# A feed-forward tail woven on VectorE: gate products between the quantiser's steps, a pass moved to ScalarE, a lag of three groups

## The reference

```python
x = x + attention(_layernorm(x), ln_gamma, ln_beta, w_qkv, w_out, b_out)   # 16 heads of 64, rotary, softmax
def fp4_quant_dequant(x):            # blocks of 16 along the last axis
    scale = max(abs(xb)) / 6.0;  scale = maximum(scale, 1e-12)
    xn = xb / scale
    q = GRID[searchsorted(MID, abs(xn))] * sign(xn) * scale     # GRID 0 .5 1 1.5 2 3 4 6
def fp4_linear(x, w): return fp4_quant_dequant(x) @ fp4_quant_dequant(w).T
y = _layernorm(x)
h = silu(fp4_linear(y, w_gate)) * fp4_linear(y, w_up)
x = x + fp4_linear(h, w_down)
```

## Time and profile before

| engine | busy us | share of the span |
|---|---|---|
| TensorE | 1506.3 | 95% |
| GpSimd | 1353.2 | 85% |
| VectorE | 1155.6 | 73% |
| ScalarE | 896.9 | 56% |

### The profile page before, as it was taken

One profiled execution on the slowest core, in us unless ns is written; L12 is line 12 of the kernel. 1 busy time (PEld: TensorE's weight loads), 2 busy tenths in 40 slices (PEclk: granted clock), 3 DMA queues, 4 the chain that ended last, 5 costly groups with the idle time before them and its releaser, 6 DMA issues.

```text
span 1588.7 us, 25645 instructions
## 1 busy us (share of the span) xinstructions
PE 1506.3 (95%) x9257; PEld 789.0 (50%) x9257; DVE 1155.6 (73%) x1562; ACT 896.9 (56%) x1383; POOL 1353.2 (85%) x793
## 2 busy tenths in 40 slices
PE   3799999999999999999999999999999999998677
PEld 1345555455555555545545454555545445554455
DVE  4777777677777777777777777777777777764687
ACT  1266566665665665756656666665655665663222
POOL 4589999789889989899889999999889899975774
PEclk9699999999999999999999999999999999999798
DMA  5111111111111111111111111111111111100001
GB/s 133 44 28 48 48 39 48 48 43 43 33 48 46 37 48 48 40 48 47 43 37 39 48 34 48 48 39 48 48 48 43 28 48 46 32 17 23 7 14 33
DMA packets 69197, 67.10 MB, mean 42 GB/s; under 512 B 26512, under 2 KB 52432, under 8 KB 69072
## 3 DMA queue, kind: packets, MB, share of 16 engines
q1 hardware_dynamic: 69072, 65.46, 16.3%
HBM read 29.25 MB, written 2.62 MB: 20 GB/s over the span
## 4 chain that ended last, share of the span: by engine, by line
PE 90%; DVE 7%; issue 2%; ACT 1%; DMA 0%; ACTq 0%; DVEq 0%
PE po L1131 30%; PE st L1118 24%; PE mx L1173 10%; PE ms L1154 8%; PE ms L1142 4%; PE ms L1199 4%; PE ms L1190 4%; PE mx L1258 1%; PE ms L1181 1%; PE st L1258 1%; DVE probs L827 1%; DVE st L821 1%; DVE negmax L872 1%; DVE probs L1023 0%; ACT xnT L618 0%
## 5 line engine op out<-in xcount | busy, mean ns | idle before, releaser
L385 POOL TENSOR_TENSOR psum_keys<-psum_keys,probs 128x1024 f32<-128x1024 f32 x256 | 609.5, 2381 | 99.6 <-ACT probs L640 80.0
L640 ACT ACTIVATE probs<-st 128x1024 f32<-128x1024 f32 x512 | 497.9, 1028 | 131.8 <-PE st L1118 127.2
L1131 PE MATMUL po<-probs,v 128*64 128x512 f32 x2048 | 495.9, 605 | 0.0
L872 DVE TENSOR_REDUCE negmax<-mx 128x2 f32<-128x1024 f32 x318 | 388.6, 1222 | 126.0 <-PE mx L1173 125.8
L874 DVE TENSOR_REDUCE negmax<-mx 128x1 f32<-128x512 f32 x186 | 128.7, 692 | 214.0 <-PE mx L1173 214.0
L1131 PEld LDWEIGHTS po<-probs,v 128*64 128x64 f32 x2048 | 124.2, 136 | 256.2 <-issue 172.0
L1173 PE MATMUL mx<-keys_hi,queries_hi 64*128 64x512 f32 x1008 | 226.8, 446 | 8.6 <-ACT max_copy L668 5.4
L1118 PE MATMUL st<-queries_hi,keys_lo 64*128 64x512 f32 x1024 | 202.7, 392 | 0.0
L1118 PE MATMUL st<-queries_lo,keys_hi 64*128 64x512 f32 x1024 | 202.0, 391 | 0.0
L1118 PE MATMUL st<-queries_hi,keys_hi 64*128 64x512 f32 x1024 | 201.4, 390 | 0.0
L385 POOL TENSOR_TENSOR psum_keys<-probs 128x1024 f32<-128x1024 f32 x64 | 152.7, 2385 | 34.8 <-ACT probs L640 34.8
(11 more groups left out here) (161 smaller groups left out, 1750.6 us busy)
## 6 DMA issues: line engine op xcount, KB each, us to landing
kq<-sin_part SPq DMA_DIRECT2D x256, 128.0 KB, 2.4
rsum<-recips SPq DMA_DIRECT2D x128, 128.0 KB, 3.0
wqkv<-in_L_attn_w_qkv_dram SPq DMA_DIRECT2D x32, 192.0 KB, 2.9
resid<-in_L_attn_x_dram SPq DMA_DIRECT2D x4, 512.0 KB, 8.1
wout<-in_L_attn_w_out_dram SPq DMA_DIRECT2D x32, 64.0 KB, 2.6
out_dram<-resid SPq DMA_DIRECT2D x8, 256.0 KB, 2.3
sums<-sums_kept SPq DMA_DIRECT2D x64, 4.0 KB
spread<-sums SPq DMA_DIRECT2D x64, 4.0 KB, 1.6
```

The costliest lines, as they stand in the source:

```text
L385: nc.gpsimd.tensor_tensor(psum_keys[:, c], first, probs[:, (STEPS * P + i) % RING], ALU.add)\
L640: nc.scalar.activation(probs[:, step_n % RING], st[step_n % 2][:, :], ACT.Exp, scale=SCALE)\
L872: nc.vector.tensor_reduce(out, banks[:, :], AX.X, ALU.max, negate=True).then_inc(mx_free, 1)
L1131: last = mm(po[HD * a:HD * a + HD, :], v[:, P % 2, KEY_ORDER[jt], HD * a:HD * a + HD], probs[:, step_n % RING, a], start=(jt == 0), stop=( ...
```

## The change

Four things, all in the feed-forward tail:

1. VectorE's order. The gate products of group g+1 are put between the quantiser's steps of group g: tiles 0 and 1 ahead of the block scales of g, tiles 2 and 3 between the scales and the multiplication. `tanh` has two tiles of room in place of four, `h_all` has four buffers in place of three.
2. The exponents are a `tensor_tensor` with a mask that is broadcast from one PSUM column; the constants are made by ScalarE in two passes over 128 x 1408, `Relu(e - 1)` and `ROUND_C * that + ROUND_C`, which stand in ScalarE's order one group later (`constants_h(g - 1)` at the end of its group g).
3. `down(g)` is issued one group later (at g+3) and is cut in two halves, one on either side of the next group's gate and up products. Tiles go in pairs: both transposes, then both projections. The last y transposes stand in groups 5 and 6 behind the first half. `down(4)` to `down(7)` come after the last gate and up products.
4. Group 7 is rounded on VectorE in two halves of 704 columns, its constants in PSUM; TensorE may start on the first half.

The steps of the last layer norm keep their order on GpSimd; on VectorE the maxima and reciprocals of `y` move behind the quantiser's multiplication of groups 2 and 3.

```diff
-            round_and_scale(h_all[g % 3], h_exp[q], h_scale[:, q], GT * FFN // BLOCK).then_inc(hq_done, 1)
+            round_and_scale(h_all[g % 4], h_exp[q], h_scale[:, q], GT * FFN // BLOCK).then_inc(hq_done, 1)
...
+        def constants_h(g, q):
+            if g == 0:
+                act.wait_ge(rounding_done, 1)
+            act.wait_ge(h_exp_done, g + 1)
+            nc.scalar.activation(h_exp[q], h_exp[q], ACT.Relu, bias=rounding[:, 0:1]).then_inc(h_two_done, 1)
+            act.wait_ge(h_two_done, g + 1)
+            nc.scalar.activation(h_exp[q], h_exp[q], ACT.Identity, bias=rounding[:, 1:2], scale=ROUND_C)\
+              .then_inc(h_val_done, 1)
...
@@ ScalarE @@
         def group(g, q):
             gate_tanh(g, (2, 3))
+            if g > 2:
+                copy_hT(g - 3, (0, 1))
+            if g in (GROUPS - 3, GROUPS - 2):
+                y_evac(g + 1)
+            if g == 3:
                 normalise_y(GROUPS - 2)
                 normalise_y(GROUPS - 1)
             if g < GROUPS - 1:
                 gate_tanh(g + 1, (0, 1))
-            if g > 1:
-                copy_hT(g - 2)
+            if g > 2:
+                copy_hT(g - 3, (2, 3))
+            if g > 0:
+                constants_h(g - 1, 1 - q)
...
@@ VectorE @@
+        def gated(g, tiles):
+            for t in tiles:
...
+                if t == 0:
+                    wait(dve, hT_ps, GT * (g - 3))
...
+        def values(g, q):
+            link(scaled(h_all[g % 4], h_all[g % 4], GT * FFN // BLOCK, h_recip))
+            wide = [PART, GT * FFN]
+            nc.vector.tensor_tensor(h_exp[q].bitcast(I32), h_all[g % 4].bitcast(I32),
+                                    h_mask.bitcast(I32).broadcast_to(wide), ALU.bitwise_and).then_inc(h_exp_done, 1)
+
+        def own_rounding(g, q):
+            n = 2 * FFN
+            dve.wait_ge(h_exp_done, GROUPS)
+            link(nc.vector.tensor_scalar(h_amax, h_scale[:, q], 1.0, None, ALU.mult))
+            for half in range(2):
...
+                link(nc.vector.scalar_tensor_tensor(last_exp, h_exp[q][:, cols], 1.0, h_round.broadcast_to([PART, n]),
+                                                    ALU.max, ALU.mult))
+                round_and_scale(h_all[g % 4][:, cols], last_exp, h_amax[:, blocks], n // BLOCK).then_inc(h_own_done, 1)
...
+        def group(g, q):
             if g < GROUPS - 1:
+                gated(g + 1, (0, 1))
+            if g == 1:
+                output_half(1)
+            if g > 2:
+                add_residual(g - 3)
+            scales(g, q)
+            if g < GROUPS - 1:
+                gated(g + 1, (2, 3))
+            if g == 0:
+                filled(dve, ("S", PAIRS - 1, 1))
+            values(g, q)
+            if g == GROUPS - 1:
+                own_rounding(g, q)
                 add_residual(g - 2)
             if g == 1:
                 seed_shift(ln_rstd, batch_rows(BATCH - 1), BATCH + 2)
                 seed(ln_rstd, batch_rows(BATCH - 1))
+            if g == 2:
+                maxima_y(GROUPS - 2)
+                maxima_y(GROUPS - 1)
+            if g == 3:
+                reciprocals_y(GROUPS - 2)
+                reciprocals_y(GROUPS - 1)
             if g == 3:
                 last_exponents(GROUPS - 2)
+            if g == 4:
+                last_exponents(GROUPS - 1)
...
+        gated(0, (0, 1))
+        nc.vector.memset(h_mask.bitcast(I32), EXPONENT)
...
+        reciprocals(PAIRS - 1, 1)
+        gated(0, (2, 3))
+        output_half(0)
+        over_groups(group)
...
@@ TensorE @@
+        def down(g, tiles):
+            if tiles[0] == 0:
+                if g < GROUPS - 1:
+                    pe.wait_ge(hq_done, g + 1)
+                if g < GROUPS - 2:
+                    wait(pe, y_done, g)
+                else:
+                    pe.wait_ge(h_done, GT * GROUPS)
+            for t in tiles:
+                if g == GROUPS - 1 and t % 2 == 0:
+                    pe.wait_ge(h_own_done, t // 2 + 1)
+                if t % 2 == 0:
+                    transpose_h(g, t)
                     transpose_h(g, t + 1)
...
         def group(g, q):
             gate_and_up(g, (2, 3))
-            if g < 2:
-                output_projection(PAIRS - 1, g)
+            if g == 0:
+                output_projection(PAIRS - 1, 0)
+            if g > 2:
+                down(g - 3, (0, 1))
+            if g in (GROUPS - 3, GROUPS - 2):
+                last_y(g + 1)
             if g < GROUPS - 1:
                 gate_and_up(g + 1, (0, 1))
-            if g > 1:
-                down(g - 2)
+            if g == 1:
+                output_projection(PAIRS - 1, 1)
+                read_out(pe, ("O", PAIRS - 1, 1))
+            if g > 2:
+                down(g - 3, (2, 3))
...
-        over_groups(group, {4: lambda: last_y(GROUPS - 2), 5: lambda: last_y(GROUPS - 1)})
-        down(GROUPS - 2)
-        down(GROUPS - 1)
+        over_groups(group)
+        for g in (GROUPS - 3, GROUPS - 2, GROUPS - 1):
+            down(g, range(GT))
```

More of the change, by code:

```diff
@@ L119, in block_program @@
     qscale = sb("qscale", [PART, 72])
+    rounding = sb("rounding", [PART, 2])
     wgT = sb("wgT", [PART, FFN])
@@ L147, in block_program @@
     halves = [st[0][:, c] for c in range(2)]
+    last_exp = st[1][:, :].rearrange("p c n -> p (c n)")[:, 0:2 * FFN]
     gate_up, hT_banks, down_banks = [mx, st[1]], [ms, halves[1]], [po, mx[:, 0], mx[:, 1]]
+    h_mask, h_round = (halves[0][:, 2 * PART + i:2 * PART + i + 1] for i in range(2))
     h_amax, h_recip = (halves[0][:, i * PART:i * PART + GT * FFN // BLOCK] for i in range(2))
@@ L729, in gate_tanh, with copy_hT @@
                 wait(act, gu_ps, n + 1)
-                nc.scalar.activation(tanh_all[:, t * FFN:(t + 1) * FFN], gate_up[n % 2][:, 0, 0:FFN], ACT.Tanh,
+                nc.scalar.activation(tanh_tiles[n % 2], gate_up[n % 2][:, 0, 0:FFN], ACT.Tanh,
                                      scale=0.5).then_inc(tanh_done, 1)
-        def copy_hT(g):
+        def copy_hT(g, tiles):
             kn = KSL[2][1]
-            for t in range(GT):
+            for t in tiles:
                 wait(act, hT_ps, GT * g + t + 1)
@@ L755, in _ @@
         gate_tanh(0, (1,))
-        over_groups(group, {4: lambda: y_evac(GROUPS - 2), 5: lambda: y_evac(GROUPS - 1)})
-        copy_hT(GROUPS - 2)
-        copy_hT(GROUPS - 1)
+        over_groups(group)
+        copy_hT(GROUPS - 3, range(GT))
+        copy_hT(GROUPS - 2, range(GT))
+        copy_hT(GROUPS - 1, range(GT))
     @block.vector
@@ L1008, in _, with scales @@
         dve.wait_ge(key_part, 4 * PAIRS)
[L1011 to L1015, removed]
+        def gated(g, tiles):
+            for t in tiles:
+                n = GT * g + t
+                e, h = tanh_tiles[n % 2], h_all[g % 4][:, t * FFN:(t + 1) * FFN]
                 gate, up = (gate_up[t % 2][:, half] for half in range(2))
-                if t == 2 and g > 2:
-                    add_residual(g - 3)
-                if g == 0 and t == 1:
+                if t == 0:
+                    wait(dve, hT_ps, GT * (g - 3))
+                if n == 1:
                     dve.wait_ge(key_sum, keys_added(PAIRS, 0))
                     dve.wait_ge(pv_ps, STEPS * PAIRS)
-                wait(dve, tanh_done, GT * g + t + 1)
+                wait(dve, tanh_done, n + 1)
                 link(nc.vector.scalar_tensor_tensor(h, e, 1.0, gate[:, 0:FFN], ALU.add, ALU.mult))
                 nc.vector.scalar_tensor_tensor(h, h, 0.5, up[:, 0:FFN], ALU.mult, ALU.mult).then_inc(h_done, 1)
-            if g < 2:
[L1026 to L1036, removed]
+        def scales(g, q):
             wait(dve, h_done, GT * g + GT)
@@ L1063, in add_residual @@
               .then_inc(y_done, 1)
-        over_groups(gated)
+        gated(0, (0, 1))
+        nc.vector.memset(h_mask.bitcast(I32), EXPONENT)
+        nc.vector.memset(h_round, ROUND_C)
+        link(nc.vector.memset(rounding[:, 0:1], -1.0))
+        nc.vector.memset(rounding[:, 1:2], ROUND_C).then_inc(rounding_done, 1)
+        reciprocals(PAIRS - 1, 1)
+        gated(0, (2, 3))
+        output_half(0)
+        over_groups(group)
         for g in range(GROUPS - 2, GROUPS):
@@ L1265, in transpose_h @@
                 last = nc.tensor.transpose(hT_banks[t % 2][0:kn, c * PART:(c + 1) * PART],
[L1266 removed]
+                                           h_all[g % 4][:, t * FFN + k0:t * FFN + k0 + kn], ident[:, :])
             last.then_inc(hT_ps, 1)
[L1269 to L1280 removed]
+        def down(g, tiles):
[6 more added lines that the diff above has]
+                    pe.wait_ge(h_done, GT * GROUPS)
+            for t in tiles:
+                if g == GROUPS - 1 and t % 2 == 0:
+                    pe.wait_ge(h_own_done, t // 2 + 1)
+                if t % 2 == 0:
+                    transpose_h(g, t)
                     transpose_h(g, t + 1)
@@ L1286, in down @@
                               start=(c == 0), stop=(c == 2))
-            last.then_inc(down_ps, 1)
```

(2 more changed lines are left out.)

40 lines of the change are left out of this document (12 added, 28 removed).

## The result

The changed kernel takes 1580.1 us (median of six runs, 1579.1 to 1581.4) against 1590.8 (six runs, 1589.1 to 1591.4): a ratio of 0.9933, 95% interval 0.9923 to 0.9944, 10.7 us faster. The forecast was 1586.2, with 1580.5 as the lower end of its range.

A forecast was written before the change was run, and what follows sets the result against it. VectorE was taken to lead in the last 132 us, with the gain coming from its waits. Mark 7 13.2 us earlier and a tail 9.0 longer gained 4.2 to 4.3 from 1590.5: 1586.2 us, range 1580.5 to 1593.5.

The forecast's parts named there:

- The tail: From mark 7 to the end of the span: 31.9 us against 22.9 before, 9.0 worse.
- values after mark 7: Group 6's multiplication and mask, 3.3 us, come after group 7's last gate product; ScalarE 2.8 and GpSimd 9.1 follow.
- idle TensorE: In the tail, after down(5), TensorE waits about 5 us for the last product of round_h(6).
- half clock: In the tail, a half-speed TensorE stretch adds 2.2 us to down(6) and down(7), 13.0 together.
- group 7's own rounding: In the tail it ends 18 to 19 us after mark 7 and is hidden; rounding in halves saves nothing.
- The new stall at the seed: VectorE's seed at the end of group 1 waits for GpSimd's variance behind round_h(0): 3.4 us lost, bounds 2.6 to 3.6.
- The y steps: Last layer norm: maxima 1.4 us, y(6) scaling wait 1.25, exponents and constants 2.1 for y(6), 2.5 for y(7).
- the marks: Mark k is the end of group k's gate products; mark 7 was forecast at 1552.6, 13.2 us earlier.
- The plain cycle of VectorE: VectorE's work per group: multiplication and mask, two pairs of tiles, residual and scales, 11.4 us.
- TensorE's loop: Four tiles of gate and up products plus a down per group: 11.1 us beside VectorE's 11.4.
- The start: From tile 1 of group 0 at 1457.7, small writes and a reciprocal about 0.2 us each, mark 1 at 1469.85.
- the second rival: Cold TensorE stretches stay away, GpSimd meetings at low bounds, transposes in time: mark 7 1548.5, tail 29.8, 1580.1 us; chance 0.16.

The follow-up runs named there:

- e4: Changed kernel with group 6 also rounded by GpSimd in two halves, its constants made in halves and down(6) released half by half: 1575.1 us.
- e7: Changed kernel with five extra products of 352 columns on TensorE between down(5) and the wait for round_h(6): 1577.6 us.
- e2: Changed kernel with TensorE waiting for both halves of group 7's own rounding before its first transpose: 1580.15 us, one run.
- e6: Changed kernel with the down projections of tiles 0 and 1 of groups 0 to 3 computed twice: 1583.2 us.
- e8: e4 with the seed moved behind products of group 3, and the exponents of y(6) and y(7) behind those of groups 5 and 6: 1575.3 us.
- e1: Changed kernel with exponents and constants of groups 0 to 6 back on VectorE, SBUF to SBUF, and no pass on ScalarE: 1582.6 us.
- e10: Changed kernel with the exponents' mask in an SBUF column in place of a PSUM column: 1587.7 us.
- e5: Changed kernel with VectorE's order unwoven and the residual of g-3 added behind the mask of g: 1604.9 us.
- e9: e4 with the last layer norm's root and the scales and multiplication of y(6) and y(7) on VectorE: 1583.9 us.
- e11: e4 with e8's place for the seed and only the scales and multiplication of y(6) and y(7) on VectorE: 1574.9 us.

## Why the prediction was right in its mechanism and wrong in its size

**Right.** The tail (31.9 forecast, 31.7 measured) held term by term: values after mark 7, ScalarE, GpSimd, idle TensorE (e4), half clock (e7), group 7's own rounding hidden (e2). TensorE's idle time was 3.8 us and not 5, as `down(5)` too had stood 3.3 us and then run at half clock; that doesn't reach the end, since `down(6)` waits for GpSimd either way. The new stall at the seed came too, 3.4 us lost forecast, VectorE idle for 3.3, but its size is partly luck (point 2 below). The mask cost 1.62 as assumed, and a pass of ScalarE 1.47 against 1.38. The y steps were, if anything, under-sized. VectorE's wait and its two meetings with GpSimd, kernel after:

```profile
1511.00 0.56 DVE L1016 RECIPROCAL y_recip<-y_scale 128x32 f32<-128x32 f32 x2
...
1514.53 0.43 DVE L852 TENSOR_SCALAR y_exp<-xnT 128x512 int32<-128x512 int32 x1 [2.97 <-POOL xnT L422]
1514.99 0.43 DVE L862 TENSOR_SCALAR y_exp<-y_exp 128x512 f32<-128x512 f32 x1
...
1526.30 0.42 DVE L852 TENSOR_SCALAR y_exp<-xnT 128x512 int32<-128x512 int32 x1
...
1526.75 2.70 DVE L862 TENSOR_SCALAR y_exp<-y_exp 128x512 f32<-128x512 f32 x1
```

For y(6) I had a wait of 1.25 for the scaling alone, with GpSimd through with `round_h(2)` before VectorE came, and then 2.1 for exponents and constants. VectorE came first, at 1511.5, and `round_h(2)` ended at 1513.0; it was a wait of 3.0 and then the plain 0.9: 4.3 in all from the reciprocals to the next products at 1515.33, against 3.95. For y(7) it was 3.1 against 2.5. The lockout of the earlier trace rows came again, as 2.70.

**Wrong: the marks, which came 18.5 us earlier, not 13.2.** Three terms carry it.

1. *The plain cycle of VectorE*, "11.4 us". The last cycle, 6-7, has nothing else in it and took 10.89: 3.27 for multiplication and mask, 2.07 and 2.06 for the pairs of tiles (I had 2.2), 0.51 for the residual (0.7), 2.98 for the scales. Neighbouring instructions that don't depend on each other start some 0.1 us before the one ahead is through (1546.80 behind 1546.36 + 0.52 = 1546.88), and I had added a gap to each. With two pairs of tiles in all six cycles and a residual in four, this is 6 x 0.27 + 4 x 0.19 = 2.4 us.
2. *TensorE's loop.* Forecast 11.1 us and 12.5 with y transposes, so I had VectorE wait 0.4 in cycle 5-6 and 1.2 in 6-7 for transposes, and 0.3 in 1-2 and 0.6 in 2-3 for cold tanh. In the trace the products of group 7 start at 1540.25, directly behind the mask, 10.88 us after those of group 6 at 1529.37; the tanh waits come to 0.8 in 2-3 and 0.2 in 4-5. That is 1.6 us. e6 shows what was left: some 0.2 us of slack in cycle 3-4 and none in 6-7, where I had TensorE 1.2 us late. I had taken a stretch of products right after a restart (1.42 + 1.20 for two tiles) for every one; following straight on, two tiles take 2.37. Nor was TensorE cold behind mark 1: I had the constants of group 0 wait until mark 1 + 4.5 for the tanh of group 2, but they start directly behind the mask, timeline of the kernel after:

```profile
1473.07 1.47 ACT L752 ACTIVATE psum_keys<-psum_keys,rounding 128x1408 f32<-128x1408 f32 x1 [1.02 <-DVE psum_keys L1057]
```

That is mark 1 + 3.3. GpSimd is through with the variance at mark 1 + 18.0 and not + 19.3, VectorE is there at + 14.8 and not + 15.9. Both came over a microsecond early, so the stall between them kept its size by luck. The stall ends when GpSimd is through, so VectorE's faster cycle alone would have brought nothing up to there.
3. *The start.* Four one-column writes took 0.06 us each and not 0.2, and everything to mark 1 was 0.6 shorter.

These make 4.6 us; the y terms take back 0.9. The remaining 1.6 is in small pieces of cycles 1-2 to 5-6: the maxima of y lengthen cycle 3-4 by 1.0 and not 1.4, from mark 2 to the products behind the seed it is 6.7 and not 7.05, the output half of cycle 1-2 takes 1.4 and not 1.6; the rest is in smaller ones. The plain cycle was off by 5%, a cycle of TensorE with y transposes, 10.9 and not 12.5, by 15%. The forecast gain was the small difference of two large sums, 13.2 and 9.0, so 5 us of error on the first more than doubled it. The measured time is that of the second rival, 1580.1, but for the greater part not by its mechanism. It had the transposes in time and y(6)'s exponents free of GpSimd, and both are so; but the cold stretches that it left out did come, windows of the kernel after:

```profile
1489.30:1494.30 5.00, 4.95 (x9) 2.88 (x10) 4.66 (x8) 0.46 (x1) 4.18 (x12) 0.50 0.01 2
1516.50:1521.60 5.10, 5.05 (x10) 2.98 (x11) 4.89 (x9) 0.46 (x1) 4.94 (x4) 0.50 0.18 53
```

VectorE's scales covered them but for 0.8 and 0.2 us. Its tail, 29.8, was 1.9 too short, and its mark 7, 1548.5, still 1.2 too late with the 0.6 taken off. That its sum fits the measured time is luck.

**What the prediction didn't see.** I asked of VectorE alone whether it had idle time. GpSimd's instructions from `round_h(0)` to `round_h(6)` sum to 78 us before and after, and after the change they fill 90% of the stretch. e8 took 4.5 us out of two cycles and 3.6 came back in the others, as waits for GpSimd and TensorE. So GpSimd and VectorE are near full in this stretch and TensorE has almost no slack in its order (e6); what one gives up is lost to another, and which of them bounds the marks is not shown. A bound by each engine's total work over the woven stretch (78 for GpSimd, 76 for VectorE, in 87) would have bounded the sum from below: the 21.4 us of GpSimd's idle time say that mark 7 could come up to some 20 us earlier, an estimate from this row, so 13.2 was no ceiling.

## What to carry to other kernels

Where a forecast is the difference of a saving and a cost, size both from back-to-back starts in the trace, not from durations with a gap added, and check the walked-through order against each engine's total work in the stretch. When a stage is made to lag to let a slow engine keep up, the lag is paid at the end: cut the last item of the slow engine into pieces there (e4, 5.0 us), not the item behind it (e2, nothing). Moving work to a slower engine can pay when it keeps another from being locked out (e1, and e10 for the mask's place in PSUM), but the instruction order has to be made for it: unwoven, the same parts were 13.5 us slower than the kernel before (e5).

## What the runs showed of the hardware

- A VectorE instruction with two SBUF inputs was held up by GpSimd's, whatever its own size: 3.16 us for one on 128 x 8 elements (0.17 without), 3.88 for the mask of 128 x 1408 (1.62), and GpSimd's product was stretched from 2.59 to 3.85 when the mask was first (e9, e10). The rule of the Trainium skill, SBUF — State Buffer, section Who interferes with whom, states this lockout for two SBUF inputs, and these rows agree. What I had not expected is that moving 19 tiny instructions to VectorE makes a 4 us job one of 13 (e9).
- A `tensor_scalar` from SBUF to SBUF was held up too, with its one input: 3.16 for the constants of 128 x 1408 (0.89 without, e1), 1.73 for one on 128 x 32 in e11 (0.18 without, in e9). One operand in PSUM kept both engines at full speed in all eight mask instructions of the kernel after, 1.62 each.
- TensorE's granted clock was 0.50 behind idle times of 4.5, 4.3, 3.8 and 3.3 us in the kernel after (the last ahead of `down(5)`), and 1.00 behind one of 3.2 us: the products at 1475.61 ran at full speed. But 2.7 us of work and 2.3 us of idle time later they fell to half speed at 1481.1, in the middle of a stretch of products that had begun at 1.00. In the kernel before, a gap of 3.2 us, 1574.7 to 1577.9, did make it fall. The length of the last gap alone doesn't tell which.
